# A language-model tower on one Trainium2 core: the experts and the final sum in one part, the last two groups' results kept on chip

## The reference

```python
h = jnp.einsum('bei,eih->beh', jnp.concatenate([merged, ones], -1), w1)
h = jax.nn.gelu(h, approximate=False)
o = jnp.einsum('bej,ejo->beo', jnp.concatenate([h, ones], -1), w2)
out_tok = jnp.einsum('beo,bke->bkeo', o, vals).reshape(b, K * E, d)
out = jnp.zeros_like(x).at[jnp.arange(b)[:, None], flat_idx].add(out_tok)
...
h = h + _L0_ffn_ref(_layernorm(h, axis=-1), ...)
```

## Time and profile before

| | |
|---|---|
| time, median of 3 runs (lowest to highest) | 860.74 us (858.04 to 860.97) |
| the profiled execution: its time, its span | 861.66 us, 859.9 us |
| busy, share of the span: PE, DVE, POOL, ACT | 82%, 70%, 52%, 41% |
| mean granted clock of TensorE, share of full speed | 0.937 |
| DMA, whole span | 86.34 MB, mean 100 GB/s |

### The profile page before, as it was taken

The page is one execution under the profiler, slowest core; times in us unless marked ns, Lnnn a source line. Parts: engine busy times, 40 slices in busy tenths (PEclk is TensorE's granted clock), DMA queues, the critical chain, the costliest instruction groups (busy, mean ns, idle before and its releaser), DMA issues. The chain is left out here.

```text
span 859.9 us, 20461 instructions
## 1 busy us (share of the span) xinstructions
PE 701.9 (82%) x7740; PEld 479.6 (56%) x7740; DVE 600.9 (70%) x853; ACT 353.4 (41%) x563; POOL 447.4 (52%) x250
## 2 busy tenths in 40 slices
PE   6577679868999999999999999994899859766674
PEld 4466444436777777777777777763677524322232
DVE  3688548888999999999999999992577621000014
ACT  3366534434544455544554454542555321210000
POOL 1788400004999999999999999992122100000000
PEclk9699979997999999999999999996999969988895
DMA  4100000000001010000000000002920199999977
GB/s 113 50 2 0 0 0 0 0 0 16 14 11 37 14 37 12 10 8 12 12 12 10 9 12 12 15 15 66 401 87 2 30 367 409 413 414 421 413 313 251
DMA packets 47291, 86.34 MB, mean 100 GB/s; under 512 B 5552, under 2 KB 30704, under 8 KB 47120
## 3 DMA queue, kind: packets, MB, share of 16 engines
q1 hardware_dynamic: 43696, 83.33, 26.2%
q10 hardware_dynamic: 3552, 2.43, 0.9%
HBM read 76.31 MB, written 9.44 MB: 100 GB/s over the span
## 5 line engine op out<-in xcount | busy, mean ns | idle before, releaser
L907 POOL TENSOR_TENSOR read<-state,q_pos 128x1024 f32<-128x1024 f32 x128 | 300.3, 2365 | 28.5 <-DVE state L1016 22.4
L1016 DVE TENSOR_TENSOR_SCAN state<-fac,ps_up 128x1024 f32<-128x1024 f32 x128 | 289.9, 2277 | 8.6 <-ACT fac L951 8.6
L951 ACT ACTIVATE fac<-ps_xf 128x1016 f32<-128x1016 f32 x128 | 130.2, 1017 | 176.4 <-PE ps_xf L1050 162.8
L1050 PEld LDWEIGHTS ps_xf<-hot,xtab 64*128 64x128 f32 x2048 | 126.3, 189 | 58.0 <-ACT fac L951 43.4
L1050 PE MATMUL ps_xf<-hot,xtab 64*128 64x128 f32 x2048 | 149.2, 285 | 11.0 <-ACT fac L951 8.9
L1050 PE MATMUL ps_up<-hot,utab 64*128 64x128 f32 x2048 | 140.7, 277 | 18.3 <-DVE state L1016 18.3
L1050 PEld LDWEIGHTS ps_up<-hot,utab 64*128 64x128 f32 x2048 | 127.0, 190 | 23.8 <-issue 17.7
L916 POOL TENSOR_TENSOR utab<-tab 128x1024 f32 (+1 forms) x32 | 64.7, 2022 | 95.5 <-SPq L85 95.5
L1095 PE MATMUL ps_o<-read,sel 128*32 128x256 f32 x1024 | 82.7, 395 | 3.7 <-POOL read L907 3.7
L1669 DVE COPY h_t<-ps_ht 128x512 f32<-128x512 f32 x16 | 10.3, 686 | 86.1 <-PE ps_ht L1700 86.0
L1684 PE MATMUL ps<-w_sb,mq 128*32 128x512 f32 x256 | 38.4, 739 | 27.7 <-DMA w_sb<-in_L_ffn_w 22.6
(11 more groups left out here) (200 smaller groups left out, 953.4 us busy)
## 6 DMA issues: line engine op xcount, KB each, us to landing
w_sb<-in_L_ffn_w SPq DMA_DIRECT2D x32, 2048.0 KB, 19.2
rec_out<-osb SPq DMA_DIRECT2D x128, 32.0 KB, 1.5
ao<-rec_out SPq DMA_DIRECT2D x8, 512.0 KB, 4.1
out_dram<-h SPq DMA_DIRECT2D x8, 256.0 KB, 2.5
out_dram<-h ACTq DMA_DIRECT2D x8, 256.0 KB, 3.1
tok<-in_x SPq DMA_DIRECT2D x2, 512.0 KB, 8.1
exp_out<-eo SPq DMA_DIRECT2D x8, 128.0 KB, 18.6
oq<-exp_out SPq DMA_DIRECT2D x8, 128.0 KB, 3.0
```

The costliest lines, as they stand in the source:

```text
L907: nc.gpsimd.tensor_tensor(read[n % 2][:], state[n % 4][:].rearrange("p (b i t) -> p b i t", b=2, i=IB), q_pos[x.s][:, :, x.k].unsqueeze(2) ...
L951: nc.scalar.activation(fac[n % 2][:].rearrange("p (n t) -> p n t", t=T)[:, :, 1:], ps_x[:].rearrange("p (n t) -> p n t", t=T)[:, :, 1:], A ...
L1016: nc.vector.tensor_tensor_scan(state[n % 4][:], fac[n % 2][:], ps_u[n % 2][:], 0.0, ALU.mult, ALU.add)\
L1050: last = nc.tensor.matmul(dst[:, b * 512 + col * T:b * 512 + (col + 1) * T], stationary[rows], pos[rows], start=True, stop=True)
```

## The change

`combine` goes, and `experts` takes its work into the same block. In detail:

- All loops of the part are written out. PE reads `merged` directly, so the copies to `mq` go.
- The results of groups 0 to 5 (24 experts, `STORED`) are stored and reloaded as before, but by ACT: each store stands behind the next group's Gelu, and four reloads, each of 24 partitions by 8 KB, stand behind the last Gelu. They fill the first 24 of each 32 partitions of `oq`, which DVE has cleared.
- The result of group 6 is put into `oq` by PE and DVE: a 0/1 table `spread` (written over half of `merged`) times `eo` gives rows at their place in `ps_s`, and DVE adds them to `oq`.
- The result of group 7 never goes to `oq`. PE rearranges it (`rows_of_last`), and a second set of four matmuls for each quad adds it, with a table `last_picks` that is made while the first groups run.
- The first quad's matmuls on `oq` are issued ahead of the last half of group 7's second layer.

```diff
         def _(act):
...
+            selections(0)
+            selections(1)
+            nc.scalar.preload_act_table(ACT.Gelu)
+            def store(g):
+                act.wait_ge(eo_ok, START + g + 1)
+                act.dma_start(exp_out[QB * g:QB * (g + 1)].rearrange("x b e -> (x b) e"),
+                              eo[:, g % 2]).then_inc(eo_st[g % 2], 16)
+            for g in range(GROUPS):
+                hidden(g)
+                if 0 < g < GROUPS - 1:
+                    store(g - 1)
+                if g + 2 < GROUPS:
+                    selections(g + 2)
+            for s in range(2):
+                act.wait_ge(eo_st[s], START + 16 * (GROUPS // 2 - 1))
+            src = exp_out.rearrange("x (q j) e -> j x q e", j=QB)
+            for j in range(QB):
+                act.dma_start(oq[j * X:j * X + STORED], src[j, 0:STORED]).then_inc(f_ld, 16)
+            store_rows(act, 1)
...
         def _(dve):
...
+            for g in range(GROUPS):
+                for h in range(2):
+                    hidden(g, h)
+                if g == GROUPS - 1:
+                    dve.wait_ge(row_mm, SPREAD_MM)
+                    dve.wait_ge(f_ld, START + 16 * QB)
+                    nc.vector.tensor_tensor(oq[:], oq[:], ps_s, ALU.add).then_inc(row_ok, 1)
+                results(g)
+                if g == GROUPS - 2:
+                    dve.wait_ge(h1_mm, START + GROUPS)
+                    nc.vector.tensor_tensor(spread, at_row[:].unsqueeze(2).broadcast_to([P, B, X]),
+                                            at_expert[:].unsqueeze(1).broadcast_to([P, B, X]), ALU.mult)\
+                        .then_inc(row_ok, 1)
+            dve.wait_ge(row_mm, ROWS_MM)
+            nc.vector.tensor_copy(last_rows[:], ps_p).then_inc(row_ok, 1)
...
         def _(pe):
...
+            pe.wait_ge(m["wbias"], START + 32)
+            first_layer(0)
+            picks_of_last()
+            first_layer(1)
+            pe.wait_ge(row_ok, PICKS)
...
+            transpose_hidden(GROUPS - 1)
+            second_bias(GROUPS - 1)
+            spread_rows()
+            second_layer(GROUPS - 1, 0)
+            pe.wait_ge(row_ok, SUMS)
+            output_stored(0)
+            second_layer(GROUPS - 1, 1)
+            rows_of_last()
+            pe.wait_ge(row_ok, ROWS)
+            output_last(0)
+            for q in range(1, QUADS):
+                output_stored(q)
+                output_last(q)
```

More of the change, by code:

```diff
@@ L32 @@
 HT = HID // P
+STORED = X - 2 * QB
 EPS = 1e-5
@@ L1578, in experts @@
     eo = sb("eo", [P, 2, E])
[L1580 to L1589 removed]
+    oq = sb("oq", [P, QUADS, E])
@@ L1607, in _, with selections @@
[L1607 to L1612, removed]
-            for s in range(2):
-                hidden(TURNS - 1, s)
+            def selections(g):
+                if g > 1:
+                    act.wait_ge(l2[g % 2], START + 2 * (g // 2))
+                nc.scalar.copy(sel[g % 2][:], ident[0:X, QB * g:QB * (g + 1)].unsqueeze(2)
+                               .broadcast_to([X, QB, B])).then_inc(sel_ok, 1)
@@ L1618, in _ @@
             m["start"](sp)
[L1620 to L1632, removed]
@@ L1645, in _ @@
[L1645 to L1657, removed]
@@ new lines, in second_layer, with picks_of_last @@
+                last.then_inc(l2[s], 1)
+            def picks_of_last():
+                pe.wait_ge(row_ok, STRIP)
+                for q in range(QUADS):
+                    at = QUADS - 1 - q
+                    for j in range(QB):
+                        rows = slice(j * X, (j + 1) * X)
+                        last = nc.tensor.matmul(ps_t[rows, q], strip[rows, at:at + X], picked[rows, q],
+                                                start=True, stop=True)
+                last.then_inc(row_mm, 1)
@@ new lines, in spread_rows, with rows_of_last @@
+            def spread_rows():
+                pe.wait_ge(row_ok, SPREAD)
+                pe.wait_ge(gl, START + GROUPS)
+                for q in range(QUADS):
+                    last = nc.tensor.matmul(ps_s[:, q], spread[:, QB * q:QB * (q + 1)].rearrange("p j x -> p (j x)"),
+                                            eo[:, 0], start=True, stop=True)
+                last.then_inc(row_mm, 1)
+            def rows_of_last():
+                pe.wait_ge(eo_ok, START + GROUPS)
+                for j in range(QB):
+                    last = nc.tensor.matmul(ps_p[j * X:(j + 1) * X],
+                                            ident[:].rearrange("p (n j) -> p j n", j=QB)[:, j],
+                                            eo[:, 1], start=True, stop=True)
+                last.then_inc(row_mm, 1)
@@ L1765, in _, with output_stored @@
+            def output_stored(q):
+                if q > 1:
+                    pe.wait_ge(f_add, START + q - 1)
                 for j in range(QB):
                     rows = slice(j * X, (j + 1) * X)
-                    last = nc.tensor.matmul(ps[q % 2][:, j, 0:E], picked[rows, q], oq[rows, q], start=True, stop=True)
-                last.then_inc(f_mm, 1)
-        @block.vector
-        def _(dve):
-            for q in range(QUADS):
-                dve.wait_ge(f_mm, START + q + 1)
-                rows = h2[:, QB * q:QB * (q + 1)]
-                nc.vector.tensor_tensor(rows, ps[q % 2][:, :, 0:E], rows, ALU.add).then_inc(f_add, 1)
+                    nc.tensor.matmul(ps_q[q % 2][:, j, 0:E], picked[rows, q], oq[rows, q], start=True, stop=False)
@@ new lines, in output_last @@
+            def output_last(q):
+                for j in range(QB):
+                    rows = slice(j * X, (j + 1) * X)
+                    last = nc.tensor.matmul(ps_q[q % 2][:, j, 0:E], last_picks[rows, q], last_rows[rows],
+                                            start=False, stop=True)
+                last.then_inc(f_mm, 1)
+            pe.wait_ge(m["wbias"], START + 32)
[3 more added lines that the diff above has]
+            pe.wait_ge(row_ok, PICKS)
```

182 lines of the change are left out of this document (91 added, 91 removed).

## The result

The changed kernel takes 865.45 us (median of 6 runs, 863.31 to 867.88) where the one before takes 860.68 beside it (6 runs, 858.04 to 861.72): a ratio of 1.0061, 95% interval 1.0042 to 1.0081. It is slower by 0.6%, where no change was forecast; the profiled execution has a time of 864.09 us and a span of 862.4.

The account below looks back on a forecast made before the run. Weight transfers bound the kernel until 834.3 us, then a serial chain, then output transfers. Last half 4.9 later, 4.7 gained behind it, half clock 0.7 more: 1.0 on 860.74 gives 861.7 us, range 854.0 to 865.5.

Parts of the forecast that it names:

- The start: Part's start: without the copies to mq, PE and the weight stream begin 0.8 us earlier, bounds 0 and 1.2.
- The reload is what decides: Behind the last Gelu: the reload meets the saturated weights, and the last half starts at 839.2 against 834.3.
- four turns of some 3.2 us: Reload beside the weights: four turns, each half a weight transfer and 0.6, landing it at 835.3.
- Turns are taken in long bursts of 16 packets an engine: Two DMA queues, read from the earlier trace: they alternate in long bursts, so the reload does not overtake the weights.
- Some of that price is an empty pipe, so I take 2.2: Weight stream: 0.79 MB more stored and reloaded bytes make the last weights 2.2 us later, bounds 0 and 2.7.
- Issue and first packet: Reload's beginning: issued after the last Gelu ends at 821.6, with 0.9 us to its first packet.
- The last half: Group 7's second layer: starts at 839.2, after reload at 835.8, DVE's sum 2.5 and quad 0's matmuls 0.9.
- Behind it: Last half to first add at half clock: 3.65, copy 0.44, rearranging 1.05, copy 0.48, last four matmuls 1.27.
- Rival C: Output stage: reload late and PE's half clock lasts through the output, 2.7 more, 863.4 us; chance 0.12.
- The output: Output stage: 12.8 us from the first add, plus 0.7 for two quads at half clock.
- Rival D: ACT's stores: their issue blocks while queues are full, last Gelu and reload up to 4.4 later; chance 0.06.
- Rival A: Reload hidden: its packets get ahead of the weights, sum ready by 834, 5.8 less, 854.9 us; chance 0.22.

Follow-up runs that it names:

- e7: Changed kernel with the 32 picks' matmuls done twice, which only moves the instruction fetches; 863.81 us, ratio 1.0038.
- e8: Changed kernel with the picks' matmuls done twice and exp_out laid out so that reload packets are 8 KB; 860.4 us, ratio 0.9997.
- e1: Changed kernel without its four reloads and DVE's wait for them, results of 24 experts missing; 854.94 us, ratio 0.9942.
- g1: Changed kernel with the first six groups' results written from eo straight into oq, four transfers a group, no reload; 866.03 us, ratio 1.0079.
- e4: Changed kernel with the reload on SP's queue behind the last weights and the last half ahead of the sum; 859.24 us, ratio 1.0004.
- e3: Changed kernel with only the reload and its store waits moved to SP's queue behind the last weights; 866.36 us, ratio 1.0085.
- e2: Changed kernel with the last half and rearranging ahead of the first quad's matmuls on oq, and group 7's result ahead of DVE's sum; ratio 1.0046.
- f1: Changed kernel with the reload reading rows of w2 in place of exp_out, first 24 experts' results missing; 863.83 us.
- f3: Changed kernel with the reload reading 96 partitions of a free on-chip weight buffer, first 24 experts' results missing; 866.0 us.
- f2: Changed kernel with the reload writing 96 partitions of a free weight buffer in place of 24 of oq, first 24 experts' results missing; 860.98 us.

## Why the prediction was wrong

Forecast 861.7 us, within 0.5%; measured 865.45. The mechanism named as deciding, a reload that meets the saturated weights and is waited for, was right; how the two queues share the engines was misread from the rows, and the terms that rest on it, the reload's landing and its price for the weights, were mis-sized.

- **The start.** 0.8 us earlier, as forecast: from the end of ACT's copy to `merged` to PE's first matmul it is 0.48 us (701.21 to 701.69) and was 1.33 (702.65 to 703.98).
- **The failed step: "The reload is what decides"**, in both its numbers. The first was the landing: "four turns of some 3.2 us" were 16.5 us from the first packet at 820.76 to the last landing, 4.1 each. Behind it stands a misreading of the earlier trace rows, "Turns are taken in long bursts of 16 packets an engine". In rows 7 ACT's queue had not begun (its first packet comes at 848.50), and in rows 8 the first transfer of SP's queue was at its end. Between the two, where both had packets, they moved one for one already in the kernel before, 848.5 to 849.0:

```profile
DMA packets 188, 0.19 MB, mean 385 GB/s; under 512 B 0, under 2 KB 188, under 8 KB 188
## 3 DMA queue, kind: packets, MB, share of 16 engines
q1 hardware_dynamic: 99, 0.10, 56.9%
q10 hardware_dynamic: 89, 0.09, 51.2%
```

  With packets of 4 KB against 1 KB it is one for one as well, 64 packets on each of 12 engines at 255 ns, 16.3 us. That the turns of the prediction came within 3 us of the landing is luck. (Its "Both ways give 835.8" is 835.3 one way and 835.7 the other.)
- **The second number** was the price for the weights: "Some of that price is an empty pipe, so I take 2.2" was 5.4, more than its bound of 2.7. Bytes were counted, while the rate of all 16 engines falls from 418 to 326 GB/s: of the estimate of 5.4 us above, 3.5 are this fall and 1.9 the bytes. The rows of before show no such fall: the two queues together moved 385 GB/s in the rows above, and q1 with little else 384 in 849.45 to 850.0.
- The Trainium skill ("DMA: Bandwidth & Descriptors", section "Why a DMA increments its semaphore by 16 and not by 1") gave 12 engines for 24 partitions. The trace agrees: 13 reports, 12 and one at the issue. In the same page of the Trainium skill, the section "Queues, rings and completion order" has a DMA engine take some 9 to 17 descriptors from one queue before it turns to the next, and the prediction says that the earlier trace rows agree. They do not, as said above. If a packet of the profile is a descriptor, which no run shows, the traces differ from the page, before the change and after it (471 packets of the reload, one per 255 ns on each of 12 engines); the measurement decides.
- **Issue and first packet.** The reload was issued 3.5 us earlier than forecast, counted from PE's first matmul, and its first packet came 4.1 us after the issue instead of 0.9. They nearly cancel.
- **The last half** starts at 139.2 where the prediction has 136.1 (839.2 - 703.15): 2.9 for the reload, the rest for quad 0's matmuls, 1.24 us at half clock where 0.9 was taken.
- **Behind it** 6.1 us against 6.9 forecast: half clock for the last half (3.61), but full from 844.4 on, so rearranging and last four took 0.71 and 0.76 in place of 1.05 and 1.27. Rival C, half clock through the output, is out.
- **The output** is 1.4 longer than before, where 0.7 was forecast from half-clocked quads. The place was right and the cause another, an instruction fetch: with the fetch moved (e7, e8) it is 14.0.
- Rival D is out: ACT's issues of stores take 0.33 to 0.36 us each. Rival A's time is what e1 shows without a reload, 854.94 against 854.9, but only as a number: e1's weights land 2.4 us earlier than A's and its output is 1.8 longer.
- **The sum.** Against the kernel before: start -0.8, D +8.9, last half to first add -5.5, output +1.4: +4.0 us from the two traces, where the interval of the ratio is 3.6 to 7.0. The profiled execution is 1.4 us below its median, and its part begins early. Against the forecast: 3.1 late at the last half, 0.8 less behind it, 0.7 more in the output, 3.0 of the 3.75 us by which the median of 865.45 misses 861.7.

One slip of the text ahead: of the 32 weight transfers 8, not 16, are issued before the part begins. No term used it.

What stays open: why neighbouring destination partitions slow also the weight packets of engines that carry no reload, whether the tensor has a part in it, and e7's late weights.

## What to carry to other kernels

A small transfer beside a saturated stream is not priced by its bytes: look at how many DMA engines its partitions give it and at where it lands, because the big transfer ends with its slowest engine (g1: 7.4 us for 768 packets of 1 KB). Before a rule for two queues is read from a window, make sure that both have packets in all of it; two windows half a microsecond away from the right one misled the prediction here. Before a chain is cut, ask what the earlier work has to wait for in its new place: here 5.5 us were gained behind the last weights and 8.9 lost ahead of them. What need not be there early goes behind the stream on the same queue, and the work that waits for it behind the work that does not (e4, 5 us); either alone (e3, 1.0085, and e2, 1.0046) left the kernel slower than before.

## What was not expected of the hardware

- Two queues that write SBUF at once move less together than one alone when one writes a few neighbouring partitions: 265 GB/s with 16, 326 with 24, 360 with 24 spaced by four, 375 with 96, 416 to 418 alone. With 24 it was seen in four more executions, 322 (f1), 325 (e2), 322 (e7) and, with SBUF as source, 331 (f3); the other rates are from one execution each.
- Weight packets of 159 ns were all stretched in that time: in 822 to 832 only one in a hundred took less than 178 ns. So those of the 4 of 16 engines that had no packet of the reload must have been stretched too.
- Two queues that both have packets on a DMA engine take turns packet by packet: 99 against 89 with 1 KB each (before), 758 against 754 with 4 KB and 1 KB (f2).
- A fetch of one 16 KB block of instructions holds one DMA engine 0.9 to 1.2 us in the changed kernel, and 0.96 to 1.71 in the outputs of all kernels; in the output that lengthens the last stage from 14.0 us to between 15.2 and 15.8 (e2's 16.4 has quads at half clock in it).
